# Edge softmax of a graph attention layer: transpositions in place of products with the identity, and the mask applied by GpSimd

## The reference, cut to what matters

```python
kj = k[src] + e                                   # e = edge_attr @ We
alpha = jnp.einsum('ehc,ehc->eh', q[dst], kj) / jnp.sqrt(C)
amax = jax.ops.segment_max(alpha, dst, num_segments=n)
ea = jnp.exp(alpha - amax[dst])
denom = jax.ops.segment_sum(ea, dst, num_segments=n)
out = segment_sum((v[src] + e) * ea / denom[dst], dst)
```

## Time and profile before

| what | value |
|---|---|
| median of 3 runs | 2856.69 us (2856.47 to 2860.34) |
| profiled execution, its own time | 2858.14 us |
| its span | 2856.4 us |
| PE (TensorE matmul) busy | 2554.0 us, 89% |
| PEld (TensorE weight load) busy | 2169.2 us, 76% |
| DVE (VectorE) busy | 2039.5 us, 71% |
| POOL (GpSimd) busy | 1711.9 us, 60% |
| ACT (ScalarE) busy | 1549.3 us, 54% |
| edge loop, first to last keys block | 350.0 to 2164.9 us |

### The profile page before, as it was taken

One profiled execution on the slowest core, in us unless ns is written; L12 is line 12 of the kernel. 1 busy time (PEld: TensorE's weight loads), 2 busy tenths in 40 slices (PEclk: granted clock), 3 DMA queues, 4 the chain that ended last, 5 costly groups with the idle time before them and its releaser, 6 DMA issues. The chain is left out here.

```text
span 2856.4 us, 67306 instructions
## 1 busy us (share of the span) xinstructions
PE 2554.0 (89%) x13731; PEld 2169.2 (76%) x13732; DVE 2039.5 (71%) x5145; ACT 1549.3 (54%) x4293; POOL 1711.9 (60%) x2023
## 2 busy tenths in 40 slices
PE   1599699999999999999999999999996747999980
PEld 0244588888888888888888888888884737999980
DVE  2655788888888888888888888888886872111116
ACT  1001266666666666666666666666664224666650
POOL 3000377777777777777777777777775213555540
PEclk9999899999999999999999999999998559999995
DMA  6132577677777767777777767777762532222218
GB/s 212 36 110 105 178 215 207 207 210 212 207 210 207 206 204 207 207 209 214 208 207 208 207 204 210 209 211 211 206 202 73 158 114 61 71 70 70 70 61 270
DMA packets 304076, 490.12 MB, mean 172 GB/s; under 512 B 52058, under 2 KB 217692, under 8 KB 303580
## 3 DMA queue, kind: packets, MB, share of 16 engines
q0 software_dynamic: 81152, 259.63, 31.7%
q1 hardware_dynamic: 215548, 214.12, 23.6%
q10 hardware_dynamic: 7056, 12.85, 1.4%
HBM read 435.86 MB, written 51.41 MB: 171 GB/s over the span
## 5 line engine op out<-in xcount | busy, mean ns | idle before, releaser
L744 POOL DMA_INDIRECT kv_ring<-vk_table,idx_c x880 | 880.0, 1000 | 654.4 <-issue 242.7
L881 PE MATMUL ps_e<-we_sb,aT 128*128 128x256 f32 x3520 | 910.2, 381 | 11.0 <-DVE kqq L971 9.4
L965 DVE TENSOR_TENSOR ve_ke<-kv_ring,ps_e 128x512 f32<-128x512 f32 x880 | 603.4, 686 | 181.7 <-PE ps_e L884 111.2
L881 PEld LDWEIGHTS ps_e<-we_sb,aT 128*128 128x128 f32 x3520 | 602.3, 191 | 58.6 <-issue 9.0
L815 ACT COPY aT<-ps_t 128x256 f32<-128x256 f32 x880 | 326.8, 371 | 468.8 <-PE ps_t L869 334.9
L754 POOL TENSOR_TENSOR w_ring<-ve_ke,ea 128x264 f32<-128x264 f32 x880 | 562.7, 640 | 30.3 <-PE ps_u L934 10.0
L934 PE MATMUL ps_u<-w_ring,sel 128*128 128x264 f32 x1760 | 548.6, 394 | 6.6 <-DVE acc L1031 3.7
L884 PE MATMUL ps_e<-q_sb,selT 128*128 x1760 | 524.6, 380 | 0.0
L1031 DVE TENSOR_TENSOR acc<-acc,ps_u 128x264 f32 x880 | 370.0, 420 | 24.8 <-DVE acc L1019 11.7
L954 DVE TENSOR_REDUCE alpha<-kqq 128x8 f32<-128x256 f32 x880 | 367.9, 418 | 7.2 <-issue 5.2
L884 PEld LDWEIGHTS ps_e<-q_sb,selT 128*128 128x128 f32 x1760 | 335.4, 191 | 46.0
(11 more groups left out here) (250 smaller groups left out, 2669.0 us busy)
## 6 DMA issues: line engine op xcount, KB each, us to landing
a_ring<-in_edge_attr SPq DMA_DIRECT2D x880, 128.0 KB
loc_c<-loc_table SPq DMA_DIRECT2D x55, 512.0 KB
kv_ring<-vk_table,idx_c POOLq DMA_INDIRECT x880
vk_table<-kv_out SPq DMA_DIRECT2D x49, 256.0 KB, 2.0
got<-y_table ACTq DMA_DIRECT2D x49, 256.0 KB, 3.8
skip_table<-skip_out SPq DMA_DIRECT2D x49, 128.0 KB, 1.7
skip<-skip_table SPq DMA_DIRECT2D x7, 896.0 KB, 7.1
xn_table<-acc SPq DMA_DIRECT2D x7, 896.0 KB, 4.9
```

Source lines behind the costliest of these rows:

```text
L744: g.indirect_dma_start(out=kv_ring[:, i % N_KV, :], out_offset=None, in_=vk_table, in_offset=bass.IndirectOffsetOnAxis(ap=idx_c[:, par, i: ...
L881: t.matmul(ps_e[i % 2][:, 0:D], aT[i % 2][:, k * P:(k + 1) * P], we_sb[:, k, :], start=(k == 0), stop=(k == KD - 1))
L965: v.tensor_tensor(both, kv.rearrange("p (t h c) -> p t h c", t=2, c=C), by_head(e, C)[:, None, :, :].to_broadcast([P, 2, H, C]), ALU.add). ...
```

## The change

Three blocks of TensorE are written with transpose in place of matmul, the scores are combined with the mask by GpSimd in the new step apply_mask (part 5 of its order), and the copy spread_mask on ScalarE goes. The transposition of key_prev and min_l is 128 columns wide and is issued first; the two behind it overwrite all but its last 8 columns. The two outputs ranked are written over not_f and not_l.

```diff
@@ gpsimd
+                def apply_mask(c, par):
+                    pool.wait_ge(s["alpha_ready"], at("alpha_ready", c * CH - 1))
+                    pool.sem_inc(s["pool_pace"], 1)
+                    pool.wait_ge(s["scores_turned"], at("scores_turned", c - 2))
+                    g.tensor_tensor(by_head(am[:, :], H), mask[:, bass.ds((c - 1) * CH, CH)][:, :, None].to_broadcast([P, CH, H]),
+                                    by_head(alpha[1 - par][:, :], H), ALU.subtract).then_inc(s["am_ready"], 1)
+
                 def emit(c, par, steps):
                     held = None
                     for kind, i, back in steps + [("end", 0, 0)]:
+                        if kind == "mask":
+                            if held is not None:
+                                gather(c, par, held)
+                                held = None
+                            apply_mask(c, par)
+                            continue
...
-                over_chunks(pool, emit, what="weigh")
+                over_chunks(pool, emit, what="weigh", parts={5: "mask"})
@@ scalar
-                        elif kind == "mask":
-                            act.wait_ge(s["scores_turned"], at("scores_turned", c - 2))
-                            act.sem_inc(s["act_pace"], 1)
-                            nc.scalar.copy(by_head(spread_mask[:, :], H),
-                                           mask[:, bass.ds((c - 1) * CH, CH)][:, :, None].to_broadcast([P, CH, H])
-                                           ).then_inc(s["mask_spread"], 1)
...
-                over_chunks(act, emit, what="select", parts={0: "mask", 3: "apart", 4: "offs", 11: "exp"})
+                over_chunks(act, emit, what="select", parts={3: "apart", 4: "offs", 11: "exp"})
@@ tensor, keys
-                            t.matmul(ps_k[:, 0:P], run[:, 0:1].to_broadcast([P, P]), ident[:, :], start=True, stop=True)
-                            t.matmul(ps_k[:, P:2 * P], run[:, P - 1:P].to_broadcast([P, P]), ident[:, :], start=True, stop=True)
-                            t.matmul(ps_k[:, 2 * P:KW], key_prev[:, 0:1].to_broadcast([P, P]), ident[:, P - H:P],
-                                     start=True, stop=True).then_inc(s["keyed"], 1)
+                            t.transpose(ps_k[:, KW - P:KW], key_prev[:, 0:1].to_broadcast([P, P]), ident[:, :])
+                            t.transpose(ps_k[:, 0:P], run[:, 0:1].to_broadcast([P, P]), ident[:, :])
+                            t.transpose(ps_k[:, P:2 * P], run[:, P - 1:P].to_broadcast([P, P]), ident[:, :]).then_inc(s["keyed"], 1)
@@ tensor, scores
-                            pe.wait_ge(s["alpha_ready"], at("alpha_ready", c * CH - 1))
-                            pe.wait_ge(s["mask_spread"], at("mask_spread", c - 1))
+                            pe.wait_ge(s["am_ready"], at("am_ready", c - 1))
                             pe.wait_ge(s["keys_apart"], at("keys_apart", c - 1))
-                            t.matmul(ps_a, alpha[1 - par][:, :], nident[:, :], start=True, stop=False)
-                            t.matmul(ps_a, spread_mask[:, :], ident[:, :], start=False, stop=True).then_inc(s["scores_turned"], 1)
+                            t.transpose(ps_a, am[:, :], ident[:, :]).then_inc(s["scores_turned"], 1)
@@ tensor, minima
-                            t.matmul(ps_r[:, 0:P], scan_b[:, 0:1].to_broadcast([P, P]), ident[:, :], start=True, stop=True)
-                            t.matmul(ps_r[:, P:2 * P], scan_f[:, P - 1:P].to_broadcast([P, P]), ident[:, :], start=True, stop=True)
-                            t.matmul(ps_r[:, 2 * P:KW], min_l[par][:, 0:1].to_broadcast([P, P]), ident[:, P - H:P],
-                                     start=True, stop=True).then_inc(s["min_spread"], 1)
+                            t.transpose(ps_r[:, KW - P:KW], min_l[par][:, 0:1].to_broadcast([P, P]), ident[:, :])
+                            t.transpose(ps_r[:, 0:P], scan_b[:, 0:1].to_broadcast([P, P]), ident[:, :])
+                            t.transpose(ps_r[:, P:2 * P], scan_f[:, P - 1:P].to_broadcast([P, P]), ident[:, :]).then_inc(s["min_spread"], 1)
@@ vector, own (the same for not_l)
-                        v.tensor_tensor_reduce(out=ranked[:, :], in0=ps_r, in1=not_f[:, :], scale=1.0, scalar=BIG, op0=ALU.add,
+                        v.tensor_tensor_reduce(out=not_f[:, :], in0=ps_r, in1=not_f[:, :], scale=1.0, scalar=BIG, op0=ALU.add,
```

More of the change, by code:

```diff
@@ L611, in gnn_ffn @@
             ea = [sb3(f"ea{i}", [P, P]) for i in range(2)]
-            spread_mask = sb3("spread_mask", [P, P])
+            am = sb3("am", [P, P])
             resets = [sb3(f"resets{i}", [P, P + 1]) for i in range(2)]
@@ L618, in gnn_ffn @@
             not_l = sb3("not_l", [P, KW])
-            ranked = sb3("ranked", [P, KW])
             scan_f = sb3("scan_f", [P, P])
@@ L638, in gnn_ffn @@
                                     alpha_ready=0, apart_ready=0, sel_ready=0, apartT_ready=0, selT_ready=0, weighted=2 * CH, summed=2 * CH, acc_added=2,
-                                    mask_spread=0, keyed=0, keys_apart=0, key_kept=0, offs_ready=0,
+                                    am_ready=0, keyed=0, keys_apart=0, key_kept=0, offs_ready=0,
                                     scores_turned=0, scanned_f=0, scanned=0, min_spread=0, owned_f=0, owned=0, least1_ready=0,
@@ L994, in softmax @@
                         dve.sem_inc(s["softmax_pace"], 1)
-                        v.tensor_tensor_reduce(out=ranked[:, :], in0=ps_r, in1=not_l[:, :], scale=1.0, scalar=BIG, op0=ALU.add,
+                        v.tensor_tensor_reduce(out=not_l[:, :], in0=ps_r, in1=not_l[:, :], scale=1.0, scalar=BIG, op0=ALU.add,
                                                op1=ALU.min, accum_out=min_l[1 - par][:, :]).then_inc(s["owned"], 1)
```

## The result

The changed kernel takes 2810.95 us (median of 4 runs, 2808.66 to 2812.57) against 2858.49 us (2856.47 to 2860.34) for the kernel before: a ratio of 0.9833, with a 95% interval from 0.9816 to 0.985. That is 47.5 us less, where 51.6 were forecast. Its profiled execution has a time of 2812.57 us and a span of 2810.8 us.

A forecast was written before the change was run, and what follows sets the result against it. TensorE's instruction stream was taken to bound the edge loop. Savings of 55.6 us less 4 us for late am gave 51.6 us off the profiled 2858.1, 2806.5, or 2805 us against the runs' median; range 2797 to 2828.

The forecast's parts named there:

- The bound: Edge loop: TensorE's instruction stream sets the time, busy 1110.00 of 1110 us, so time taken from it comes off.
- The blocks: TensorE's keys, minima and scores as transpositions: 0.35, 0.35 and 0.33 us saved, 1.03 us a chunk.
- the term of 55.6 us: Edge loop: 1.03 us saved a chunk over 54 distances between chunks.
- The price of am: GpSimd's new 128x128 mask operation: about 365 ns, between 0.27 and 0.64 us, plus 0.2 us for the handoff.
- The order on GpSimd: Behind gather 5: am, weigh, then gather 6, which moves about 0.4 us later, covered by VectorE's later use.
- Late am: TensorE's scores wait for am when a GpSimd gap stands shortly before gather 5: 4 us in all, between 0 and 14.
- The chunk that was named: Chunk of the last GpSimd gap, gather 5 ending at 1938.80: TensorE would wait 2.0 us for am before scores.
- the tail: The 55th set of blocks, after the last item: counted as nothing, could give or cost a few tenths of a us.
- VectorE as the next bound: Items 6 to 10: VectorE takes over, the minima's 19 us are lost, 2824 us; 8% together with late gather 6.
- A late gather 6 in every chunk: GpSimd's gather 6 delayed 0.4 us without cover: 20 us back, 2825 us; 8% together with VectorE taking over.
- Slower by late am: Scores wait for am in every chunk; slower from 2.1 us for operation and handoffs, 2880 us at 2.5; 3%.
- The clock: TensorE's clock falls to 1.2 GHz around the blocks because of more transpositions: +263 us, 3120 us; 1%.

The follow-up runs named there:

- kernel 5: The changed kernel with three more copies of GpSimd's mask operation ahead of the real one, into spare tiles: 2863.50 us, ratio 1.0015 to the kernel before.
- 1, keys and minima only: The kernel before with only the keys and minima blocks as transpositions, scores, spread_mask and GpSimd unchanged: 2826.41 us, ratio 0.9885.
- 9, changed again: The changed kernel run once more with nothing altered, beside other versions: 2814.02 us, ratio 0.9838 to the kernel before.
- 3, mask ahead: The changed kernel, but GpSimd's mask step no longer flushes the held gather, so am comes before gather 5: 2809.30 us, ratio 0.9831.
- 10, mask ahead again: The version with GpSimd's mask step ahead of the held gather, run again beside the changed kernel: 2808.68 us, ratio 0.9823.
- kernel 6: The changed kernel with the mask operation on VectorE and GpSimd's order as before the change: 2807.81 us, ratio 0.9819.
- kernels 7 and 11: One edge product replaces two in turn_scores: 2797.60 us on the version with GpSimd's mask ahead, 2796.12 us on that with the mask on VectorE.

## Why the prediction was right

**The bound.** That TensorE's stream sets the time held in each experiment: passes taken out came off at their distance between starts, at four places (keys, scores, minima, turn_scores), alone and together.

**The blocks.** Keys and minima went from 0.68 to 0.33 us, scores from 0.44 to 0.11, as worked out, to within 0.01. The ordinary chunk lost 1.02 us where the sum had 1.03, so the term of 55.6 us stands at 54.9. That the wide transposition of key_prev is no loss stands too; it is worth 0.06 us a block over a narrow product put first.

**The price of am.** 414 ns and not 365, between the bounds of 270 and 640. It mattered little: 0.84 us of slack were left in the ordinary chunk.

**The order on GpSimd: the step that failed.** The prediction had am followed by "weigh, then gather 6", with gather 6 some 0.4 us late. It is two weighs, and gather 6 is 0.76 us later behind gather 5 than before. And it didn't ask who waits for the weigh behind am: TensorE's very next sum does, so the new step has two deadlines 0.11 us apart. In the ordinary chunk both are met, which is why the forecast wasn't hurt; kernel 5 shows what the second costs when they aren't.

**Late am.** Forecast at 4 us from seven gaps, between 0 and 14. Putting the mask ahead gave 4.1 and 6.3 us in the loop. That the term came out so near is partly luck. The chunk that was named has TensorE 1.9 us late before the scores (1.73 us of it shown as idle time), and 2.0 were forecast. But the other six gaps together gave only 0.4 to 0.5 us there, where 2 were forecast, and the 1.9 to 2.0 us that make up the sum were lost before the next sums, to the weigh that the forecast did not have as a deadline.

**What was not counted.** The loop gave 46.3 us of 55.6. The starts of the 55 keys blocks of each trace say where the rest went. The ordinary chunk is the median distance, and "longer chunks" adds up what the chunks above the median take beyond it.

| trace | loop, us | ordinary chunk | first chunk | longer chunks |
|---|---|---|---|---|
| before | 1814.9 | 33.67 | 30.17 | 1.8 |
| 1, keys and minima only | 1780.2 | 32.99 | 29.46 | 3.9 |
| changed | 1768.6 | 32.65 | 30.93 | 8.8 |
| 9, changed again | 1766.7 | 32.65 | 30.50 | 7.3 |
| 3, mask ahead | 1762.3 | 32.65 | 30.21 | 3.2 |
| 10, mask ahead again | 1762.6 | 32.65 | 30.98 | 2.6 |

In the changed kernel 0.7 us is the rounding of the price (54.9 and not 55.6). Some 1.8 us is the first chunk, which was 3.5 us under the ordinary one before and is 1.7 under it now; it varies between kernels and between executions of one kernel, so this part can't be put down to the blocks. The other 7.0 us stand in longer chunks, nearly all of them those of GpSimd's gaps or right behind one: 4.3 are late am and the weigh behind it, 1.5 is TensorE late before projections (2.6 us in place of 1.2), and the rest is in small pieces. The lateness before projections is 1.3 us in the second trace of the same kernel and 0.9 and 1.6 with the mask ahead, so it isn't clear that it grew. VectorE's waits for gathered rows grew (4.7 us before, 10.3 in kernel 1, 6.9 to 13.4 with the whole change), which fits the gaps being caught up with less spare time a chunk. Where the time is lost is shown; that the gaps cause it is argued, since no experiment took them away.

**Slips in the prediction's readings.** The seven gaps were put at 3 to 3.5 us; in the trace of before they are 2.8 to 3.65. The lower end of its own range, 2798 us, does not follow from its terms: 2856.7 - 55.6 is 2801, and the tail was allowed a few tenths. Neither touches the forecast.

**The rivals.** VectorE as the next bound: not here, nor with one more operation on it (kernel 6). A late gather 6 in every chunk: it is 0.76 us later, yet VectorE waited for a gathered row 16 and 11 times in the two traces, not in each of 55 chunks. Slower by late am: its mechanism is real, and its point of decision was sized at an am that takes 2.1 us; four operations, 1.49 us from the first start to am's end, were already enough to lose everything, since the second deadline adds to the first. The clock: the granted clock is 1.00 in the loop with 40 transpositions a chunk. The sentence of the Trainium skill (TensorE: Matmul & The Clock Gate, section "Part 4: PE-mode transpose") that transposition mode does not bring the full clock did not matter here. The transpositions run at 1.00, but 132 of the 172 passes of a chunk are products, so no run shows what transpositions alone would do.

## What to carry to other kernels

When one engine is full, price its work by the distance between starts and take passes out of it: a transposition of float32 is one pass where the product with the identity is two. When the work goes to another engine, write out that engine's new order, step by step with its loop indices, and ask for each instruction behind the new one who waits for it and when; the cost is decided by the deadline and not by the load. Put the new step where its inputs have just become ready, not behind a wait that it doesn't need. And compare the ordinary turn of a loop (the median) beside its mean: here it gave the price to 0.01 us a chunk, and showed that the missing time lay in a few chunks.

## What the runs showed of the hardware that was not expected

A pass of 8 columns costs about as much as one of 128. A single narrow product hides this: its two passes take 0.13 to 0.14 us together, since the second starts only 0.03 us behind the first, and what follows is up to 0.04 us (a transposition) or 0.09 us (a sum of 264 columns) late. In turn_scores, with two narrow products in a row, the passes are 0.11 us apart from the second on, and taking one product out gave 0.22 us, 0.11 a pass (kernels 7 and 11). So a transposition of 128 columns, 0.11 us, is cheaper than a product of 8.

GpSimd's gaps are not spread at random. In the kernel before they stand ahead of gathers 113, 223, 333 and so on to 773, counted from 0: every 110th. The gaps ahead of the first four of these are there in all thirteen traces, 2.8 to 3.65 us long; the later ones take 1.15 to 4.2 us, by the kernel. Of the seven only 773 is an item 5, which is why one chunk carries most of the late am. What GpSimd does in them no run shows.

GpSimd's 128x128 operation takes 414 ns, 49 ns above the line through its own 264 and 1792 element rows. The same operation on VectorE has a record of 312 ns on average (median 285) in kernel 11:

```profile
L979 DVE TENSOR_TENSOR am<-mask,alpha 128x128 f32<-128x128 f32 x55 | 17.2, 312 | 0.0
```
